# Tridiagonalization of a 256 x 256 matrix: squares summed before the dots, A x corrected before u, beta and what follows from it behind the products

## The reference, cut to what matters

```python
# four layers, each x = layernorm(x + layer(x)), on x (32, 256, 128) and adj (256, 256)
deg = jnp.sum(A, axis=0) + jnp.sum(A, axis=1) - jnp.diagonal(A)
d_inv_sqrt = jnp.where(deg > 0, jax.lax.rsqrt(deg), 0.0)
L = jnp.diag(deg) - A
L_norm = d_inv_sqrt[:, None] * L * d_inv_sqrt[None, :]
_, U = jnp.linalg.eigh(L_norm)
agg = jnp.einsum('mn,bnd->bmd', U.T, features)
```

## Time and profile before

| | |
|---|---|
| median of 3 runs | 3087.7 us (3087.53 to 3089.22) |
| the profiled execution | 3087.03 us |
| its span, first to last instruction | 3085.4 us |
| tridiagonalization, two-tile half (24 to 729 us) | 705 us |
| tridiagonalization, one-tile half (729 to 1303 us) | 574 us |
| PE, DVE, ACT, POOL busy over the span | 61%, 70%, 26%, 8% |
| mean granted TensorE clock | 0.813 |

### The profile page before, as it was taken

How to read it: one execution, slowest core, us unless ns; L and a number is a source line. 1 busy time by engine, 2 the same in 40 slices (tenths; PEclk the granted TensorE clock), 3 DMA queues, 4 the chain that set the end, 5 groups by cost and what they waited for, 6 DMA issues and landing times. The chain is left out here.

```text
span 3085.4 us, 45879 instructions
## 1 busy us (share of the span) xinstructions
PE 1872.0 (61%) x11008; PEld 1629.7 (53%) x11008; DVE 2158.4 (70%) x12407; ACT 812.4 (26%) x3204; POOL 255.3 (8%) x367
## 2 busy tenths in 40 slices
PE   5777777777777777600000031386878878779777
PEld 5666666666666666600000020265667667667666
DVE  6777777777777777799999999675454454454453
ACT  1111111112222222220000010153434435435434
POOL 0000000000000000032232230021010010010010
PEclk9888898889999999955555555688889889889888
DMA  0000000000000000010000000011000000000000
GB/s 24 1 1 1 1 1 1 1 1 1 1 1 1 1 1 1 1 46 0 1 0 1 1 1 1 7 54 55 1 14 11 2 14 10 3 14 10 3 7 7
DMA packets 23034, 23.04 MB, mean 7 GB/s; under 512 B 1584, under 2 KB 19664, under 8 KB 22736
## 3 DMA queue, kind: packets, MB, share of 16 engines
q1 hardware_dynamic: 20304, 13.15, 1.5%
q0 software_dynamic: 2560, 8.39, 0.8%
HBM read 13.15 MB, written 8.39 MB: 7 GB/s over the span
## 5 line engine op out<-in xcount | busy, mean ns | idle before, releaser
L273 PE MATMUL bank<-const 128*128 128x128 f32 x2816 | 425.1, 288 | 0.0
L273 PEld LDWEIGHTS bank<-const 128*128 128x128 f32 x2816 | 385.4, 206 | 0.0
L323 PE MATMUL bank<-Qp,const 128*128 128x128 f32 x512 | 130.1, 337 | 301.7 <-DVE Qp L471 301.6
L726 DVE SCALAR_TENSOR_TENSOR q<-rec,nb,q 128x14 f32<-128x14 f32 (+1 forms) x1270 | 277.0, 257 | 0.0
L323 PEld LDWEIGHTS bank<-Qp,const 128*128 128x128 f32 x512 | 79.7, 196 | 352.1 <-DVE Qp L471 352.1
L1458 ACT ACTIVATE gate<-bank,gbias 128x128 f32<-128x128 f32 (+3 forms) x576 | 209.0, 432 | 177.7 <-PE bank L1413 136.9
L722 DVE RECIPROCAL rec<-q 128x14 f32<-128x14 f32 (+1 forms) x1270 | 247.2, 236 | 11.8 <-DVE q L726 1.4
L351 ACT ACTIVATE nrm<-nx,tiny 128x1 f32<-128x1 f32 x256 | 75.4, 294 | 644.3 <-DVE nx L421 644.3
L833 PE MATMUL bank<-tq,const 128*128 128x1 f32 x2 | 0.6, 362 | 367.1 <-DVEq L913 367.1
L317 PE MATMUL bank<-R,A 128*128 128x128 f32 x1280 | 222.6, 314 | 0.7 <-DVE A L507 0.4
L317 PEld LDWEIGHTS bank<-R,A 128*128 128x128 f32 x1280 | 198.9, 228 | 3.1 <-DVE A L507 3.0
(11 more groups left out here) (370 smaller groups left out, 4550.4 us busy)
## 6 DMA issues: line engine op xcount, KB each, us to landing
xnext<-in_x SPq DMA_DIRECT2D x16, 256.0 KB, 3.5
x_scratch<-x1out POOLq DMA_DIRECT2D x16, 256.0 KB, 3.6
xin<-x_scratch SPq DMA_DIRECT2D x16, 256.0 KB, 2.8
out<-yout POOLq DMA_DIRECT2D x16, 256.0 KB, 2.8
const<-in_consts SPq DMA_DIRECT2D x1, 1495.5 KB, 6.4
adjN<-in_adj SPq DMA_DIRECT2D x1, 256.0 KB, 6.6
wqkv<-in_L_gnn_Wqkv SPq DMA_DIRECT2D x1, 192.0 KB, 7.5
W<-in_L_gnn_W SPq DMA_DIRECT2D x2, 64.0 KB, 3.5
```

Of the source, the lines that this page charges most:

```text
L273: mm(banks[7][:, 0, 0:P], ones, ident1, start=True, stop=True)
L323: mm(pG[:, own], ones, Qp[:, own], start=True, stop=True).then_inc(h_g, 1)
L726: done[side] = ch.mark(v.scalar_tensor_tensor(q[:, r, 0:points], rec[:, side, 0:points], nb2[:, max(r, r + side):max(r, r + side) + 1], q[ ...
```

## The change

TensorE: in both halves the squares now stand ahead of the dots. The keep-warm matmuls are 3 behind A x and 3 behind the sums in the two-tile half (2 and 2 before), 6 and 3 in the one-tile half (3 and 4 before), and 3 new ones stand at each panel's end between the transposes and the update. VectorE: one order for both halves. `Ec` comes behind `nx`; `zr`, the product A x less its correction, is made as soon as tau is there, ahead of u; `Au` and `Qp` follow u; hh, rtau, beta, p, `bR`, zz and `uA` come behind `Qp`. ScalarE: the next unit vector is copied ahead of beta's copies in both halves. What is computed is the same; matmuls of constants apart, no instruction is added or taken away.

```diff
--- before.py
+++ after.py
@@ -303,12 +303,8 @@
                                        start=(t == heads[0]), stop=(t == heads[-1]))
 
                             pe.wait_ge(h_e, k + 1)
-                            if lone:
-                                squares()
-                                x_dots()
-                            else:
-                                x_dots()
-                                squares()
+                            squares()
+                            x_dots()
 
                             if j == 0:
                                 pe.wait_ge(h_A, blk + (first // PANEL + 1))
@@ -317,11 +313,11 @@
                                     last = mm(pZ[:, u, 0:PC], A[:, t, u * P:(u + 1) * P], R[:, t, 0:PC],
                                               start=(t == tiles[0]), stop=(t == tiles[-1]))
                             last.then_inc(h_z, 1)
-                            keep_warm(3 if lone else 2)
+                            keep_warm(6 if lone else 3)
 
                             pe.wait_ge(h_q, k + 1)
                             mm(pG[:, own], ones, Qp[:, own], start=True, stop=True).then_inc(h_g, 1)
-                            keep_warm(4 if lone else 2)
+                            keep_warm(3 if lone else 3)
 
                         pe.wait_ge(h_p, blk * PANEL + (first + PANEL))
                         pe.wait_ge(h_w, blk * PANEL + (first + PANEL))
@@ -331,6 +327,7 @@
                         for t in tiles:
                             last = nc.tensor.transpose(pPe[0:2 * PANEL, 0, t * P:(t + 1) * P], Pe[:, t, :], ident1)
                         last.then_inc(h_T, 1)
+                        keep_warm(3)
                         pe.wait_ge(h_Tc, blk * 2 + (2 * first // PANEL + 2))
                         c0 = tiles[0] * P
                         for t in tiles:
@@ -342,7 +339,7 @@
                 A_ = nc.scalar.activation
                 A_(R[:, :, EC:PC], unit[:, :, 1:2], ACT.Copy).then_inc(h_e, 1)
                 for first, tiles in PHASES:
-                    here, lone = slice(tiles[0], T2), len(tiles) == 1
+                    here = slice(tiles[0], T2)
                     with nc.scalar.Fori(0, BLOCKS) as blk:
                         for j in range(PANEL):
                             k = blk * PANEL + (first + j)
@@ -351,20 +348,14 @@
                             A_(nrm[:, :], n2, ACT.Sqrt, bias=tiny[:, :]).then_inc(h_nrm, 1)
                             A_(half_n2[:, :], n2, ACT.Copy, scale=0.5).then_inc(h_half, 1)
 
-                            def next_unit():
-                                act.wait_ge(h_z, k + 1)
-                                A_(R[:, here, EC:PC], unit[:, here, bass.ds(k + 2, 1)], ACT.Copy).then_inc(h_e, 1)
-
                             act.wait_ge(h_u, k + 1)
-                            if lone:
-                                next_unit()
+                            act.wait_ge(h_z, k + 1)
+                            A_(R[:, here, EC:PC], unit[:, here, bass.ds(k + 2, 1)], ACT.Copy).then_inc(h_e, 1)
                             act.wait_ge(h_b, k + 1)
                             A_(nbeta[:, :], beta, ACT.Copy, scale=-1.0).then_inc(h_nb, 1)
                             A_(kept[:, bass.ds(k, 1), :], stat[:, :].unsqueeze(1), ACT.Copy)
                             A_(V[:, here, bass.ds(k, 1)], u_col, ACT.Copy)
                             A_(Pe[:, here, 2 * j:2 * j + 1], u_col, ACT.Copy).then_inc(h_pe, 1)
-                            if not lone:
-                                next_unit()
 
                         act.wait_ge(h_T, blk + (first // PANEL + 1))
                         A_(PdT[:, tiles[0] * P:N], pPd[0:2 * PANEL, 0, tiles[0] * P:N], ACT.Copy).then_inc(h_Tc, 1)
@@ -415,11 +406,9 @@
                                 return ch.mark(v.tensor_tensor(Ec[:, here, :, 0:w], Pe[:, here, 0:w].unsqueeze(2).broadcast_to([P, nt, 2, w]),
                                                                dots[:, 0:2, at - w:at].unsqueeze(1).broadcast_to([P, nt, 2, w]), ALU.mult))
 
-                            if j and not lone:
-                                i_E = correction()
                             dve.wait_ge(h_s, k + 1)
                             v.tensor_reduce(nx[:, :], pS[:, own].rearrange(by_sum, c=2), AX.X, ALU.add).then_inc(h_n2, 1)
-                            if j and lone:
+                            if j:
                                 i_E = correction()
                             dve.wait_ge(h_n2, k + 1)
                             i_sgn = ch.mark(v.tensor_scalar(sgn[:, :], x0, 0.0, 0.5, ALU.is_ge, ALU.subtract))
@@ -434,55 +423,38 @@
                             ch.reach(i_nrms)
                             i_tau = ch.mark(scaled(tau, n2s[:, :], inv[:, :], nrms[:, :]))
 
-                            def Ax():
-                                dve.wait_ge(h_z, k + 1)
-                                if j:
-                                    ch.reach(i_C)
-                                    return ch.mark(v.tensor_tensor(zr[:, here, :], pZ[:, here, XC:PC], Cc[:, here, :], ALU.subtract))
-                                return ch.mark(v.tensor_copy(zr[:, here, :], pZ[:, here, XC:PC]))
-
-                            if lone:
-                                i_zr = Ax()
+                            dve.wait_ge(h_z, k + 1)
+                            if j:
+                                ch.reach(i_C)
+                                i_zr = ch.mark(v.tensor_tensor(zr[:, here, :], pZ[:, here, XC:PC], Cc[:, here, :], ALU.subtract))
+                            else:
+                                i_zr = ch.mark(v.tensor_copy(zr[:, here, :], pZ[:, here, XC:PC]))
                             ch.reach(i_tau)
                             scaled(u, e, tau, x).then_inc(h_u, 1)
+                            ch.reach(i_zr)
+                            i_Au = ch.mark(scaled(Au[:, here], r, tau, z))
                             i_hh1 = ch.mark(v.scalar_tensor_tensor(hh1[:, :], tau, 0.5, x0, ALU.mult, ALU.add))
                             i_om = ch.mark(v.tensor_tensor(om[:, :], tau, x0, ALU.add))
-                            if lone:
-                                ch.reach(i_zr)
-                                i_Au = ch.mark(scaled(Au[:, here], r, tau, z))
-                            i_rtau = ch.mark(v.reciprocal(rtau[:, :], tau))
-                            ch.reach(i_hh1)
-                            dve.wait_ge(h_half, k + 1)
-                            i_hh = ch.mark(scaled(hh[:, :], hh1[:, :], tau, half_n2[:, :]))
-                            if not lone:
-                                ch.reach(i_hh)
-                                v.reciprocal(beta, hh[:, :]).then_inc(h_b, 1)
-                                dve.wait_ge(h_b, k + 1)
-                                ch.reach(i_rtau)
-                                i_bR = ch.mark(v.tensor_tensor(bR[:, :], beta, rtau[:, :], ALU.mult))
-                                ch.reach(i_bR)
-                                dve.wait_ge(h_u, k + 1)
-                                i_uA = ch.mark(v.scalar_tensor_tensor(uA[:, here], u, bR[:, :], below_h, ALU.mult, ALU.mult))
-                                i_zr = Ax()
-                                ch.reach(i_zr)
-                                i_Au = ch.mark(scaled(Au[:, here], r, tau, z))
                             ch.reach(i_Au)
                             dve.wait_ge(h_u, k + 1)
                             v.tensor_tensor(q_by_tile, R[:, here, XC:PC + w + 2:PC + w + 1 - XC],
                                             Au[:, here].unsqueeze(2).broadcast_to([P, nt, 2]), ALU.mult).then_inc(h_q, 1)
-                            if lone:
-                                ch.reach(i_hh)
-                                v.reciprocal(beta, hh[:, :]).then_inc(h_b, 1)
-                                dve.wait_ge(h_b, k + 1)
-                                ch.reach(i_rtau)
-                                i_bR = ch.mark(v.tensor_tensor(bR[:, :], beta, rtau[:, :], ALU.mult))
+                            ch.reach(i_hh1)
+                            dve.wait_ge(h_half, k + 1)
+                            i_hh = ch.mark(scaled(hh[:, :], hh1[:, :], tau, half_n2[:, :]))
+                            i_rtau = ch.mark(v.reciprocal(rtau[:, :], tau))
+                            ch.reach(i_hh)
+                            v.reciprocal(beta, hh[:, :]).then_inc(h_b, 1)
+                            dve.wait_ge(h_b, k + 1)
                             v.tensor_scalar(p, Au[:, here], beta, None, ALU.mult).then_inc(h_p, 1)
-                            if lone:
-                                ch.reach(i_bR)
-                                i_uA = ch.mark(v.scalar_tensor_tensor(uA[:, here], u, bR[:, :], below_h, ALU.mult, ALU.mult))
+                            ch.reach(i_rtau)
+                            i_bR = ch.mark(v.tensor_tensor(bR[:, :], beta, rtau[:, :], ALU.mult))
                             dve.wait_ge(h_p, k + 1)
```

(5 more changed lines are left out.)

## The result

The changed kernel takes **2966.6 us** (median of 4 runs, 2961.73 to 2967.82) against 3087.6 (median of 4, 3081.82 to 3089.22): a ratio of 0.9608 with an interval of 0.9592 to 0.9625. It is 121 us faster. The forecast was 3024 with a range of 2998 to 3058: the direction is right, the size is off by nearly half of the gain, and the time lies outside the range.

What follows compares the result with a forecast made beforehand. The prediction took handovers between TensorE and VectorE, chiefly VectorE's chain u to `Qp`, as the bound, the clock second. 43 + 15 + 6 = 64 us off 3087.0 gave 3023.0, stated as 3024 for the median; range 2998 to 3058.

Steps and rivals of the forecast that it cites:

- The path, u to `Qp`: Two-tile column: VectorE's chain from u to `Qp` takes 0.41 us instead of 1.67, so `Qp` comes 0.95 earlier.
- The loss by squares first: Two-tile column: squares ahead of dots delay `Ec` and A x, so u comes at 2.33 instead of 2.02, 0.31 lost.
- The column of 4.54: Two-tile column: 2.74 up to `Qp` plus 1.80 to the next `xx`, 0.41 less than 4.95; 43 us over 104 columns.
- The slow columns: Two-tile half: three cold columns a block vanish as TensorE's 1.6 us idle gap closes, 15 us gained.
- "The first two columns after a panel's end keep their length": Start of each block: the clock still falls there, so these columns are taken as unchanged; otherwise 16 us gained.
- The panel's end, 6 us: Update matmuls at seven panel ends: 1.09 us at the full clock instead of 1.97, 6 us gained.
- The one-tile half, 0: One-tile columns: 0.04 x 128 = 5 us gained against 9 lost by keep-warms; taken as 0.
- The feared 9 us of six keep-warms in the slow column: One-tile half, slow column after each of 8 panel ends: three more keep-warms delay the sums by up to 1.1 us.
- VectorE's order doesn't matter: Rival: instructions moved behind `Qp` cost all they cost before; a two-tile column of 5.34, 41 us slower, 3128; chance 0.03.
- Part of the gain: Rival: `uA` costs 0.31, cold columns remain, one-tile half loses 9; 18 us gained, near 3070; chance 0.08.
- nothing: Rival: new waits for `Ec` and A x eat all 0.41 us of the two-tile column's gain; chance 0.04.
- The clock falls and stays: Rival: all 104 two-tile columns run at 1.2 GHz, 6.5 us or more each; 148 us slower, 3235; chance 0.05.

Runs made afterwards that it cites:

- the three steps: The changed kernel with three more VectorE steps, whose results nobody reads, between u and `Au` in all 256 columns: 3020.0 us, ratio 0.9791.

## Why the prediction was right and wrong

- **The path, u to `Qp`: right.** 1.67 became 0.40 (0.41 was said), and undoing this alone gives 107 us back, nearly all of the gain. `gsum` 1.17 behind `Qp` instead of 0.74: 0.43 given back, 0.54 was said.
- **The loss by squares first: right in kind.** `nx` at 0.80 behind `xx` (0.79 was said), `Ec` at 1.25 (1.31), u at 2.22 (2.33; it was 2.02 before). The experiment with dots first shows it as a cost of 0.19 us a column.
- **The column of 4.54: wrong, 4.30 measured.** This is the step that failed first, and it is one of size. Up to `Qp` (2.74 said, 2.62 measured) two terms were too large. The slot from the dots' start to the next matmul was taken as 0.52 and is 0.45 (354.93 to 355.38). In the row that it came from the dots start only 0.03 behind their weight load and the squares 0.11 behind theirs, while now both matmuls start 0.11 behind; from weight load to weight load it is 0.44 and 0.45. And u was set 0.12 behind `zr`, as in the one-tile half; it is 0.08. From `Qp` to `xx` (1.80 said, 1.68 measured) `uA` lengthened the way from zz to zzm by 0.05 (0.26 to 0.31) and not by 0.10. `gsum` now follows zzm by 0.07 (358.05 to 358.12); the 1.26 of before held 0.15 for it, because the sums landed only at 411.52. Together 0.24 us, over 104 columns 25 us.
- **The slow columns: right**, all gone, though not for the one reason given. The new order with the old keep-warms does it, and so do the new keep-warms with the old order. Between two panel ends (408 to 460 us) the clock of the changed kernel is 1.00, as was said.
- **"The first two columns after a panel's end keep their length": wrong**, 12 us shorter (88.7 to 76.3). The prediction took the low clock as what sets their length and left the shorter path out of them. The runs show that it is the path. Here are the first two columns of the third block: the kernel before, the changed kernel with the old keep-warms, and the kernel before with the new keep-warms:

```profile
200.80:212.07 11.27, 7.13 (x44) 6.58 (x44) 7.94 (x54) 1.99 (x14) 0.00 (x0) 0.72 0.00 1
176.32:186.23 9.91, 8.32 (x41) 7.74 (x41) 6.66 (x52) 2.21 (x14) 0.00 (x0) 0.58 0.01 2
196.91:207.37 10.46, 7.33 (x48) 7.14 (x49) 7.95 (x54) 1.98 (x14) 0.00 (x0) 0.84 0.00 2
```

The second is the shortest, though its clock is the lowest. Over all eight blocks the new order with the old keep-warms takes 77.5, the old order with the new keep-warms 88.0, and the changed kernel with beta ahead again 85.5. The keep-warms added at the end are not needed for it either: without them the two columns take 76.0. The clock does still fall there in some blocks of the changed kernel, as was said: it is 0.66 in one pair of columns and 1.00 in another, 10.17 and 8.36 us long (windows above).
- **The panel's end, 6 us: right in the update** (1.97 to 1.13 at the fifth end; 1.13 at all eight now). With the last columns the ends gained 9.8. The prediction counted 13 inner columns a block and two that stay, and so put the last column's gain at nothing: at the fourth end, where the update took 1.13 before too, last column and end still went from 10.05 to 9.78. The 3.17 us behind the update stayed as said.
- **The one-tile half, 0: wrong, 17 us.** The column lost 0.11, not 0.04, which makes 13 us with columns 2 to 14. From u to `Qp` it went from 0.60 to 0.41: `Au` follows u by 0.14 instead of 0.28, the two slots of the prediction, and `Qp` follows `Au` by 0.27 instead of 0.32, which was not counted. `Qp` to `xx` went from 1.59 to 1.67. The feared 9 us of six keep-warms in the slow column have the other sign: columns 0 and 1 gained 3.9. With the old keep-warms they take 74.9 at a clock of 0.64 to 0.68 in seven of the blocks, about as before (75.1, 0.64), and 70.2 in the kernel before with the new keep-warms, so here it is the keep-warms and not the order.
- **The sum.** 43 + 15 for the inner two-tile columns, 79 measured; 6 for the ends, 10; 0 for the first two columns, 12; 0 for the one-tile half, 17. Each miss is on one side: unknown prices were taken near the dear end, and what was not worked out was put at nothing. The range was then laid around that sum, and it and the four rivals share out the whole chance, so nothing was left for a time under 2998.
- **The rivals.** VectorE's order doesn't matter: refuted by the 107 us; the three steps show why, 0.07 each. Part of the gain, and nothing: neither came. The clock falls and stays: it did not, but it is what happens without keep-warms, 3169 us.

## What to carry to other kernels

In a loop of handovers, write down for each engine the time from the loop's start to each step, and move off the chain first those steps that depend on each other: here most dependent VectorE steps cost 0.20 us and more (`Qp` behind `Au` 0.27, p behind beta 0.20), an independent one 0.07 (0.13 directly behind u). Whether an earlier start of one branch helps is set by the branch that ends last, so a change made of several moves should be tried one move at a time; here one of them cost 28 us of what the other brought. Apply what a shorter path gains to every column that runs it, also where the clock is low. And take a price from a row in which nothing waited, or subtract the wait.

## What had not been expected of the hardware

- Without any keep-warm matmul TensorE's granted clock is 0.61 and 0.50 in the two halves though it is busy for 0.74 and 0.61 of the time, and by the ratios the kernel takes 209 us more than with them. With two behind A x and two behind the sums it is 0.94 in the two-tile half; a third in each place makes it 0.97 and gains 5 to 6 us at most.
- Behind the loop's branch VectorE sits 3.17 us from the start of the A update to its next instruction, in both kernels, though the update ahead of it takes 1.13 in the one and 1.97 in the other. What fills this time the trace puts down to "issue"; it was not tried.
